# A slot plan for a gated cross-attention block: projections and weight preparation two slots later, value products 1-2-1, a ramp of 26 slots

## The reference

```python
x = x + tanh(g_xattn) * xattn(layernorm(x), ctx)      # x: 4 x 512 x 512
x = x + tanh(g_ffn)   * ffn(layernorm(x))

def xattn(hidden, cond):            # 8 groups, 2 query heads in each, d = 128
    ln_out = ln(hidden)
    q, qx, k, v = four fp8-rounded projections of ln_out   # q, qx, k: layer norm by head
    kx, vx = projections of cond                           # kx: layer norm by head
    core = softmax(q k^T / sqrt(d)) v                      # for each head
    xout = softmax(qx kx^T / sqrt(d)) vx
    return fp8(concat(core, xout) / smooth) @ wproj * scale
def ffn(x): h = bitlinear(x, w_gate_up); return bitlinear(silu(a) * b, w_down)
```

## Time and profile before

| | |
|---|---|
| median of 3 runs | 1862.5 us (1860.18 to 1867.15) |
| profiled execution, device time | 1860.7 us |
| its span, first to last instruction | 1858.9 us |
| first scores (slot 0) start | 110.0 us |
| row maximum of slot 0 / of slot 511 starts | 113.9 / 1506.1 us |
| PE busy | 1629.7 us, 88% |
| DVE busy | 1575.9 us, 85% |
| ACT busy | 1350.9 us, 73% |
| POOL busy | 1095.2 us, 59% |
| mean granted TensorE clock | 0.976 |

### The profile page before, as it was taken

The page is one execution under the profiler, slowest core; times in us unless marked ns, Lnnn a source line. Parts: engine busy times, 40 slices in busy tenths (PEclk is TensorE's granted clock), DMA queues, the critical chain, the costliest instruction groups (busy, mean ns, idle before and its releaser), DMA issues.

```text
span 1858.9 us, 35181 instructions
## 1 busy us (share of the span) xinstructions
PE 1629.7 (88%) x11164; PEld 1007.7 (54%) x11164; DVE 1575.9 (85%) x3451; ACT 1350.9 (73%) x3351; POOL 1095.2 (59%) x1421
## 2 busy tenths in 40 slices
PE   2478899788999998899899888999999879999996
PEld 1355555455656665566566555666666434444442
DVE  7569899999898899988888999999988856777774
ACT  6468998777889987898898788998988842222222
POOL 3677888876776777776777667777767530000000
PEclk9889999999999999999999999999999989999997
DMA  3357899889999998899899998999999966322200
GB/s 101 96 149 168 190 192 211 174 187 193 203 226 202 194 224 180 191 208 249 192 207 200 229 193 195 233 231 222 217 232 181 205 157 214 105 69 80 69 18 17
DMA packets 669597, 325.48 MB, mean 175 GB/s; under 512 B 552288, under 2 KB 595424, under 8 KB 669152
## 3 DMA queue, kind: packets, MB, share of 16 engines
q1 hardware_dynamic: 669408, 323.17, 77.5%
HBM read 140.61 MB, written 48.23 MB: 102 GB/s over the span
## 4 chain that ended last, share of the span: by engine, by line
PE 41%; DVE 26%; POOL 12%; ACT 8%; issue 7%; DMA 4%; SPq 1%; ACTq 0%; DVEq 0%; POOLq 0%
PE psum L699 7%; PE psum L687 6%; PE psum L654 6%; PE psum L741 6%; PE psum L716 6%; DVE pp L981 5%; DVE nmx L971 5%; PE psum L661 3%; DMA pt<-pp 3%; PE psum L758 3%; PE psum L674 2%; POOL wbt L1513 2%; POOL qk L1566 2%; ACT pp L1330 1%; POOL ars L1544 1%
## 5 line engine op out<-in xcount | busy, mean ns | idle before, releaser
L687 PE MATMUL psum<-qk 128*128 128x512 f16 x1536 | 421.9, 384 | 29.0 <-DVE pp L981 22.9
L699 PE MATMUL psum<-pt,vv 128*128 128x512 f16 x1536 | 398.5, 382 | 55.8 <-ACT cy L1338 40.6
L654 PE MATMUL psum<-wbt,xqt 128*128 128x256 f16 (+1 forms) x4096 | 411.3, 251 | 25.1 <-DVE xqt L898 11.1
L654 PEld LDWEIGHTS psum<-wbt,xqt 128*128 128x128 f16 x4096 | 333.6, 100 | 135.5 <-issue 20.4
L1319 ACT ACTIVATE psum<-psum,nmx 128x512 f32<-128x512 f32 x512 | 344.4, 673 | 84.9 <-DVE nmx L971 80.4
L981 DVE SCALAR_TENSOR_TENSOR pp<-psum,prs,pp 128x512 f16<-128x512 f32 x512 | 378.5, 739 | 5.5 <-ACT pp L1330 5.2
L971 DVE TENSOR_REDUCE nmx<-psum 128x1 f32<-128x512 f32 x512 | 344.5, 673 | 36.7 <-PE psum L687 35.2
L1330 ACT ACTIVATE pp<-psum,prs 128x512 f16<-128x512 f32 x512 | 356.7, 697 | 18.5 <-DMA pt<-pp 18.2
L699 PEld LDWEIGHTS psum<-pt,vv 128*128 128x128 f16 x1536 | 147.5, 98 | 252.5 <-issue 70.0
L1566 POOL TENSOR_TENSOR qk<-y,qk 128x512 f16<-128x512 f32 x192 | 233.7, 1217 | 16.0
L687 PEld LDWEIGHTS psum<-qk 128*128 128x128 f16 x1536 | 143.8, 99 | 114.7 <-DVE pp L981 26.0
(11 more groups left out here) (176 smaller groups left out, 2711.1 us busy)
## 6 DMA issues: line engine op xcount, KB each, us to landing
wbt<-ws SPq DMA_DIRECT2D x192, 256.0 KB, 3.8
ws<-wbt SPq DMA_DIRECT2D x64, 256.0 KB, 4.0
catd<-cy SPq DMA_DIRECT2D x64, 256.0 KB, 3.3
raw<-in_wgu SPq DMA_DIRECT2D x64, 256.0 KB, 3.6
raw<-in_w SPq DMA_DIRECT2D x32, 384.0 KB, 3.7
wbt<-catd SPq DMA_DIRECT2D x6, 2048.0 KB, 9.8
pt<-pp SPq DMA_TRANSPOSE x512, 3.7
raw<-in_wp SPq DMA_DIRECT2D x32, 256.0 KB, 3.8
```

The lines of the kernel that those rows point to most:

```text
L654: ins = e.matmul(bank[:, o0:o0 + c1 - c0], xv[:, v, kt * 512 + tt * 128:kt * 512 + (tt + 1) * 128], wb[i][:, h, kt, c0:c1], start=kt == 0 ...
L687: ins = e.matmul(SB(n), qk[i][:, jq, u, ss], qk[i][:, jk, w, :], start=k == 0, stop=k == 2)
L699: ins = e.matmul(OB, v[:, t, u, att, :], src[:, w, t, :], start=t == 0 and k == 0, stop=t == 3 and k == 2)
```

## The change

Projections (`GEMM_AT` 7 to 9), weight loads and preparation (`TILE_LOAD`, `RAMP_LOAD`, `W0_AT`, `STORE_W`, the reload of weights) and the group factors come two slots later relative to the scores. `FIRST` goes from -28 to -26, so that relative to the first slot they stand where they stood. The value products of a head are placed 1, 2, 1 in three slots, and none in the fourth, instead of 1, 1, 2. The first head of an iteration goes from slot 9 to 10; the other five keep their slots. PE starts iteration 1's projection when the four main weight tiles are done and no longer waits for the two context tiles. The loads of the second part shift by up to two slots.

```diff
-FIRST, PAST = -28, NSLOT + 20
+FIRST, PAST = -26, NSLOT + 20
-PVS = ((0,), (1,), (2, 3), ())
-GEMM_AT = 7
+PVS = ((0,), (1, 2), (3,), ())
+GEMM_AT = 9
-HEADS_AT = (9, 12, 14, 16, 18, 22)
-FACTORS_AT = 4
-TILE_LOAD = (-8, -4, -3, -1, -13, -12)
+HEADS_AT = (10, 12, 14, 16, 18, 22)
+FACTORS_AT = 6
+TILE_LOAD = (-6, -2, -1, 1, -11, -10)
...
-WG_AT, CAT_AT, X2_AT = (444, 488), (472, 496), 506
+WG_AT, CAT_AT, X2_AT = (444, 490), (474, 498), 507
...
-    "parts": (102, 102, 102, 102),
+    "parts": (104, 104, 104, 104),
...
-                nw, j = divmod(n + 8 + 2 * SLOTS, SLOTS)
+                nw, j = divmod(n + 6 + 2 * SLOTS, SLOTS)
...
-                            q.wait_ge("w_dn", it * 6 + (6 if it else 4))
+                            q.wait_ge("w_dn", it * 6 + (6 if it > 1 else 4))
```

More of the change, by code:

```diff
@@ L28 @@
 RATIO_OF = [0, 0, 1, 1, 2, 3]
-FIRST, PAST = -28, NSLOT + 20
+FIRST, PAST = -26, NSLOT + 20
 PVLAG = 9
-PVS = ((0,), (1,), (2, 3), ())
-GEMM_AT = 7
+PVS = ((0,), (1, 2), (3,), ())
+GEMM_AT = 9
 TILES = ((0, 0), (0, 1), (1, 0), (1, 1), (2, 0), (2, 1), (3, 0), (3, 1))
-HEADS_AT = (9, 12, 14, 16, 18, 22)
-FACTORS_AT = 4
-TILE_LOAD = (-8, -4, -3, -1, -13, -12)
-RAMP_LOAD = (-29, -28, -27, -22, -20, -19)
-W0_AT = -24
+HEADS_AT = (10, 12, 14, 16, 18, 22)
+FACTORS_AT = 6
+TILE_LOAD = (-6, -2, -1, 1, -11, -10)
+RAMP_LOAD = (-27, -26, -25, -20, -18, -17)
+W0_AT = -22
 PREP = {"mean": 2, "near": 3, "far": 4, "hi": 5, "lo": 6}
@@ L43 @@
 KV_PREP = {"part": 2, "mid": 6, "hi": 7, "lo": 8}
-STORE_W = 8
+STORE_W = 10
 POOL_HI = 2
 ACT_NORM = 9 * 4
-WG_AT, CAT_AT, X2_AT = (444, 488), (472, 496), 506
+WG_AT, CAT_AT, X2_AT = (444, 490), (474, 498), 507
 RAMP = -4
```

## The result

| | before | after |
|---|---|---|
| median of 19 runs each | 1862.5 us (1859.12 to 1867.15) | 1868.5 us (1863.15 to 1872.33) |
| ratio to before, 95% interval | | 1.0026 (1.0017 to 1.0035) |
| span of the profiled execution | 1858.9 | 1866.1 |
| first scores start | 110.0 | 107.0 |
| row maximum of slot 0 / 511 starts | 113.9 / 1506.1 | 110.5 / 1514.3 |

The change costs 6.0 us by the medians, 0.26% (4.9 us) by the ratio. It was forecast at 1861, practically no change, with a range of 1842 to 1880.

The account below looks back on a forecast made before the run. PE or DVE was taken to fill some iterations and no engine the other 17 (760.7 us). Terms -5 + 1 - 10 + 8 + 4 = -2 on the profiled 1860.7 gave 1858.7, with 1.8 for the median 1861 us; range 1842 to 1880.

Parts of the forecast that it names:

- Ramp, -5: Before the first scores: POOL's reordered work releases them earlier, near 104.5 to 105 us; -5 us, between -6 and -2.
- End, +1: Last slots: two projection parts from the ramp now stand in slots 487 and 488; +1 us, between 0 and +2.
- Iterations 23 to 29 at nothing: Stretch where PE is full (277.5 us): the same pieces of work sum to the same length; no change.
- DVE-full iterations at nothing: Iterations 4, 12, 13 and 20 to 22: DVE has the same instructions and hides PE's new order; no change.
- the growth of waits for transposing DMAs: Sign of being wrong: these waits were costed at nothing since their slots do not move.
- Balance, -10: 17 iterations no engine fills: evener PE slots and shorter waits for `o_out`; -10 us, range -28 to +14.
- First head behind `kv_factor`, +8: Iterations 0 to 4: PE waits for `kv_factor` before the first head, five places; +8 us, bounds 0 and +13.
- Input transposes, +4: Slots 26, 154, 282: the head moved in front shares bank 7, so PE waits 1.3 us each; +4, bounds 0 and +7.5.
- bank 7 decides: Rival: head, `kv_factor` and input transposes in one slot stop PE, and balance brings nothing; +16, 1878 us, chance 0.25.
- the ramp brings nothing: Rival: POOL's work is only reordered, so the first scores' gain is lost before slot 16; +3, 1866 us, chance 0.05.

Follow-up runs that it names:

- e4: Changed kernel with the value products back at 1, 1, 2 as the only edit; 1866.0 us.
- e6: Changed kernel with `kv_factor` ahead of the slot's statistics and normalisation on DVE; 1861.8 us.
- e9: Kernel before with only the value products placed 1, 2, 1; 1870.0 us.
- e13: Changed kernel with `kv_factor` first on DVE, the input transposes three slots earlier and the value products back at 1, 1, 2; 1848.7 us.
- e7: Changed kernel with the input transposes of slots 26, 154 and 282 three slots earlier; 1861.1 us.
- e11: Changed kernel with `kv_factor` first on DVE and the input transposes three slots earlier; 1851.5 us.
- e5: Changed kernel with the last main weight tile prepared ahead of the head's split on POOL; 1869.6 us.
- e14: Kernel before with most of the weights' low part on POOL left out for iterations 2 to 7; 1857.0 us.
- e15: e11 with most of the weights' low part on POOL left out for iterations 2 to 7; 1844.9 us.
- e10: e8 with the main weight tiles loaded one slot earlier; 1862.3 us.
- e8: Changed kernel with the edits of e5, e6 and e7 together; 1850.3 us.

## Why the prediction was off

By its own steps, with what each measured:

- **Ramp, -5:** -3.4. The mechanism was right: POOL's last split ends at 106.9 and PE is there at nearly the same time. Mis-sized was PE's work behind the first head, taken as 5.6 us with only the head at half clock; it took 8.0 us (98.47 to 106.51), because the granted clock stayed at 0.50 to 0.56 until 103.3. In e4, with the same order, it was 6.8 us, and in e6, at 0.99 and more, 5.9. The head stayed where it was, as was said, but PE waits 1.6 us for `kv_factor` in front of it; e6 takes that away.
- **End, +1:** +1.9 in iterations 30 and 31, inside the bounds (0 to +2), -1.1 behind them. The 1.89 us for a slot without projection divides 30.3 by 16, but from the row maximum of slot 496 to that of slot 511 there are 15 slots: 2.02 us, which takes 0.3 us from the term.
- **Iterations 23 to 29 at nothing:** 278.4 against 277.5. The sum of the pieces' starts held; in all the experiments this stretch took 276.3 to 279.1 us, whatever the order. The page of the Trainium skill named in the prediction (Perfetto Trace Analysis, section Identifying the Most-Contended Engine) names two measures of headroom, MFU (the share of TensorE's peak that the matmuls use) and the share of weight loads. Read by the second alone, as the prediction read it, it doesn't agree with this case: nothing in these runs found any headroom. The first was not worked out.
- **DVE-full iterations at nothing:** iteration 4 went from 53.6 to 56.2 us and 20 to 22 from 139.4 to 141.9. The prediction named this as a sign of being wrong, and the growth of waits for transposing DMAs as another: those of PE's value products went from 14.8 to 18.5 us, one of 4.0 us among them in iteration 20. Both signs came, and neither was priced.
- **Balance, -10:** -10.0 in iterations 6 to 22, with the wait for `o_out` at 26.0 where about 25 was said. That the size fits is in part luck. The term was counted over the 17 iterations that no engine fills, 0 to 3 among them, by swings that come in every four slots, but 8.5 of the 10.0 us lie in iterations 6 to 8, and 0 to 3 are longer than before. The prediction gave the gain to the change as a whole; e4, e9 and e13 show that 1-2-1 has no part in it: beside the rest of the change it is worth nothing, and alone in the kernel before it costs 7.5 us.
- **First head behind `kv_factor`, +8:** the waits are 1.6, 2.0, 2.0, 2.0 and 2.0 us in slots 10, 26, 42, 58 and 74, 9.5 in sum (9 to 11 was said). Of this, e6 gives back 4.5 in iterations 1 to 5 and 0.8 in iteration 0: 5.3 in the profiled executions, and 3.7 more in the ramp, part of which is clock.
- **Input transposes, +4:** three waits of 0.9 us, less than the 1.3 taken, but together with what they delay 4 to 7 us by e7. The kernel before had waits for L1312 there too (0.7 us in each of slots 19 and 51), which the prediction overlooked.
- **The step that failed is one that isn't there.** The sum has no term for the shift of the weight preparation in the iterations: it was put at nothing without a reason. POOL's new order was looked at only in the ramp. In iterations 1 to 5 the preparation moved past work that stayed, splits of heads and the output's subtractions on POOL, and PE's wait on L1513 went from 2.8 to 15.1 us there (9.6 to 22.1 over the whole span). These iterations lost 19.7 us; with the two priced causes taken away (e11) they are still 11.7 us longer than before. The wait on L1513 itself isn't the price, as e5 shows. About 5 us of the 11.7 go with the low part of the weights on POOL (e14, e15), and the cause of the other 6.5 stays open.

+8 and +4 were priced for iterations 0 to 4 and for 1, 9 and 17. The two repairs bring 8.0 us back in iterations 1 to 5 (e11) and 0.8 in iteration 0. But the balance brought nothing in these iterations, and its -10 was counted over them too. Had iterations 1 to 5 been costed by themselves, from POOL's and DVE's order in one of them, the unpriced 12 us could have been looked for.

The rival "bank 7 decides" (1878) named the right waits and the right direction. Its point of decision, 15 us in waits for L829 and L1312, was nearly reached (9.5 + 2.6 in iterations, 1.6 in the ramp), and e6 and e7 together are 17 us. Its +19 for the head and the input transposes meets the 18.9 us that iterations 0 to 5 lost, but the two repairs bring only 8.8 of them back, so half of that agreement is luck. It put the balance at 0, where 10 us came. The rival "the ramp brings nothing" (1866) is nearest to the measured time by luck alone: the ramp did bring 3.4 us.

## What to carry to other kernels

When two dependent pieces are moved together, their distance is kept but not their place against the work that stays: go through every in-order queue that they pass (here DVE, POOL and SP), in each kind of iteration, and ask who stands behind. Where a wait appears, try the smallest edit first, and expect no fixed price for it: letting `kv_factor` pass its neighbours in the slot was worth 6 to 7 us in the changed kernel and nothing in the kernel before, moving the input transposes away 4 to 7, and the exchange on POOL nothing. Moving heads or weight loads by a slot or more brought a new conflict each time (a shared bank, a ring of buffers, a queue of DMAs). And split a change with several parts before it is judged: a part that won in some iterations and lost in others (the shift), what came with it (two kinds of wait that two small edits repair) and a part that did nothing (1-2-1) summed to +6 us, and the change without 1-2-1 and with the two repairs (e13) is 14 us faster than before.

## What was not expected

- A wait's total says little of its price, in either direction: removing 2.6 us of waits before the input transposes was worth 4 to 7 us (e7), removing 11 us of waits for a weight tile nothing (e5), while the waits for the next instruction of the same engine rose by 11.
- A DMA that waits for its buffer stops the transposing DMAs behind it in SP's queue: moving four loads one slot earlier made the kernel 12 us slower (e10 against e8), with 14.4 us of waits of PE for the transposes in five slots and 10.5 us more of DVE's for the raw tiles.
- Without the low part of the weights on POOL (up to 1.64 us for each tile of 24), the kernel before gains only 5.5 us (e14) and e11 6.6 us (e15), though POOL is the engine for which PE waits there.
